# Moving the norm weight's scale, the last value products and the last block's output passes in a fused attention and feed-forward kernel

## What is computed

```python
x = x + _L0_xattn_ref(_layernorm(x), ctx_1024, mask, rms_scale, q_w, kv_w, out_w)   # cross attention over 1601 masked context rows
x = x + _L0_attn_ref(_layernorm(x), WQ, WK, WV, WO)                                 # causal self attention, 16 heads of 32
x = x + _L0_ffn_ref(_layernorm(x), W_fc, ln_w, ln_b, W_proj)
...
# _L0_ffn_ref
h = jnp.einsum('btd,hd->bth', x, absmean(W_fc))      # weights quantized to -1, 0, 1
h = jax.nn.gelu(h, approximate=False)
h = layernorm(h, ln_w, ln_b)                         # over 2048 features
return jnp.einsum('bth,dh->btd', h, absmean(W_proj))
```

## Time and profile before

| | us |
|---|---|
| median of 3 runs (lowest, highest) | 1093.79 (1090.33, 1094.54) |
| the profiled execution's own time | 1089.65 |
| its span | 1087.8 |
| PE busy in the span | 931.0 (86%) |
| DVE busy | 669.2 (62%) |
| ACT busy | 503.0 (46%) |
| POOL busy | 373.1 (34%) |

### The profile page before, as it was taken

The page is one execution under the profiler, slowest core; times in us unless marked ns, Lnnn a source line. Parts: engine busy times, 40 slices in busy tenths (PEclk is TensorE's granted clock), DMA queues, the critical chain, the costliest instruction groups (busy, mean ns, idle before and its releaser), DMA issues.

```text
span 1087.8 us, 22528 instructions
## 1 busy us (share of the span) xinstructions
PE 931.0 (86%) x7297; PEld 697.5 (64%) x7297; DVE 669.2 (62%) x1335; ACT 503.0 (46%) x1057; POOL 373.1 (34%) x500
## 2 busy tenths in 40 slices
PE   0898879898788888868879989998978999999995
PEld 0787757686667776657768878887754444444442
DVE  3587667766677766676266556766565447475543
ACT  2565445654455554535233233443445444556551
POOL 1354445444444444430012111221112334454533
PEclk9999999999999999979969999999988989999997
DMA  5532133221232322431355543443321202012011
GB/s 163 167 87 65 58 95 97 87 63 48 81 89 77 88 70 75 112 101 60 79 156 147 137 146 88 139 125 116 97 46 48 68 1 87 31 39 68 20 59 42
DMA packets 100608, 93.02 MB, mean 86 GB/s; under 512 B 45729, under 2 KB 62194, under 8 KB 100466
## 3 DMA queue, kind: packets, MB, share of 16 engines
q1 hardware_dynamic: 99856, 91.11, 28.9%
q10 hardware_dynamic: 578, 0.13, 0.1%
q0 software_dynamic: 32, 0.02, 0.0%
HBM read 74.37 MB, written 12.66 MB: 80 GB/s over the span
## 4 chain that ended last, share of the span: by engine, by line
PE 65%; DVE 14%; issue 10%; ACT 5%; ACTq 1%; DVEq 1%; POOL 1%; DMA 1%; SPq 1%; POOLq 0%
PE bank L245 44%; PE bank L1216 8%; PE bank L220 6%; PE bank L241 4%; DVE f L234 3%; DVE f L508 2%; ACT f L231 1%; DVEq L75 1%; ACTq L75 1%; PE bank L530 1%; ACT f L413 1%; DVE f L471 1%; DVE f L642 1%; DVE f L929 1%; PE bank L216 1%
## 5 line engine op out<-in xcount | busy, mean ns | idle before, releaser
L245 PE MATMUL bank<-f,f 128*128 128x256 f32 (+4 forms) x5032 | 635.4, 302 | 67.9 <-issue 26.3
L245 PEld LDWEIGHTS bank<-f,f 128*128 128x128 f32 (+3 forms) x5032 | 457.5, 162 | 195.7 <-issue 77.2
L220 PE MATMUL bank<-f,f 128*128 128x128 f32 x896 | 133.4, 280 | 60.1 <-DVE f L620 29.3
L234 DVE TENSOR_TENSOR f<-bank,f 128x512 fp32r<-128x512 f32 x211 | 140.7, 684 | 52.6 <-ACT f L231 50.6
L231 ACT ACTIVATE f<-bank 128x512 fp32r<-128x512 f32 x211 | 121.2, 592 | 85.6 <-PE bank L220 80.5
L220 PEld LDWEIGHTS bank<-f,f 128*128 128x128 f32 x896 | 103.6, 143 | 82.8 <-DVE f L620 31.1
L1194 POOL TENSOR_TENSOR f<-f,f 128x512 f32<-128x512 f32 x60 | 76.4, 1274 | 146.6 <-ACT f L1192 146.5
L1216 PE MATMUL bank<-f,f 128*128 128x512 f16 x512 | 124.9, 389 | 0.0
L1197 DVE SCALAR_TENSOR_TENSOR f<-bank,f,f 128x512 f16<-128x512 f32 x64 | 48.0, 750 | 107.0 <-ACT f L1184 73.5
L935 POOL TENSOR_TENSOR f<-f,f 128x512 f32<-128x512 f32 x32 | 33.4, 1045 | 182.8 <-DVE f L932 182.8
L469 POOL TENSOR_TENSOR f<-f,f 128x512 f32<-128x512 f32 x32 | 42.0, 1312 | 155.9 <-ACTq L75 133.2
(11 more groups left out here) (128 smaller groups left out, 989.0 us busy)
## 6 DMA issues: line engine op xcount, KB each, us to landing
f<-in_ctx_dram SPq DMA_DIRECT2D x71, 256.0 KB, 2.8
f<-x_scratch SPq DMA_DIRECT2D x64, 256.0 KB, 3.7
f<-in_x_dram SPq DMA_DIRECT2D x32, 256.0 KB, 3.2
x_scratch<-f SPq DMA_DIRECT2D x32, 256.0 KB, 2.1
f<-in_L_ffn_W_fc_dram SPq DMA_DIRECT2D x32, 256.0 KB, 2.8
f<-in_L_ffn_W_proj_dram SPq DMA_DIRECT2D x32, 256.0 KB, 3.5
f<-in_ktab_dram SPq DMA_DIRECT2D x71, 64.0 KB, 2.0
f<-f SPq DMA_DIRECT2D x64, 64.0 KB, 2.4
```

The costliest lines, as they stand in the source:

```text
L220: f = lambda e, i=i, a=a: e.transpose(dst[:, i, :], a, ident[0:rows, 0:rows])
L234: return maybe("dve", lambda e: e.tensor_tensor(lo, src, hi.bitcast(F32), ALU.subtract), sem(name + "_lo"), waits, when)
L245: f = lambda e, i=i, a=a, b=b: e.matmul(dst, a, b, start=(first and i == 0), stop=(last and i == n - 1), skip_group_check=check)
```

## The change

- `s3_scale` moves from slot H0-1 to slot B2+4 (order 4.6). Its small tiles move from a region that is free only late (`r`) into the constants, and its wait for that region goes to the steps that still use it (`s3_free`, `s3_rows`).
- The DVE step of `s3_apply` becomes a step of its own, `s3_turn`, at order 1.45 of the same slot: ahead of the strip's own DVE passes instead of behind them.
- For the last tile of self attention (i = 15), `s2_PV` keeps its slot s+4 = H0+6 but goes from order 0.5 to 2.6, behind strip 6 and the projection of strip 4; `s2_ET` goes to the next slot, behind strip 7; `s2_O` goes from slot s+5 to s+7.
- End: for the last strip the sum comes before the low half on DVE, and POOL's add of its squares goes; `s3_stat` of the last group adds them on PE with four more matmuls. Two tiles of strip 62's projection stand ahead of `s3_stat`, the other two behind it, then strip 63's four. For tiles 1 and 2 of the last group the first of the two DVE passes is done by ACT and POOL (`s3_mid`); the output passes go in the order of tiles 0, 3, 1, 2.

```diff
+    mrow, mdiag, isc, sc, lsc = const(2), const(2), const(2), const(2), const(2, 16)
...
-        at(s + 4, 0.5, lambda i=i: s2_PV(i))
+        at(s + 4, 0.5 if i < ni - 1 else 2.6, lambda i=i: s2_PV(i))
         at(s + 4, 0, lambda i=i: res_load(i))
-        at(s + 4, 5.5, lambda i=i: s2_ET(i))
-        at(s + 5 if i else s + 7, 5.6, lambda i=i: s2_O(i))
+        at(s + 4 if i < ni - 1 else s + 5, 5.5 if i < ni - 1 else 1.6, lambda i=i: s2_ET(i))
+        at(s + 5 if 0 < i < ni - 1 else s + 7, 5.6, lambda i=i: s2_O(i))
...
+    def s3_free():
+        tok["free"] = tok["qk", ni // 2 - 1]
+
+    def s3_turn(i):
+        u = i % 2
+        tok["tb", i] = op("dve", lambda e: e.scalar_tensor_tensor(rs2[:, u, 1:2], mv2[:, u, 0:1], -1.0, rs2[:, u, 0:1],
+                                                        ALU.mult, ALU.mult), sem("f_dv"), [tok["rs", i]])
+
     def s3_apply(i):
         u = i % 2
-        tb = op("dve", lambda e: e.scalar_tensor_tensor(rs2[:, u, 1:2], mv2[:, u, 0:1], -1.0, rs2[:, u, 0:1],
-                                                        ALU.mult, ALU.mult), sem("f_dv"), [tok["rs", i]])
...
-            tp = op("pool", lambda e: e.tensor_tensor(acc[:, v, 1, :], acc[:, v, 1, :], sq3[:, z, :], ALU.add),
-                    sem("f_acc2"), [ts, *tok["acc2", g]])
-            tok["acc2", g] = tok["sqr", z] = [tp]
+            if q == last:
+                tok["acc2", g] = [ts, *tok["acc2", g]]
+            else:
+                tp = op("pool", lambda e: e.tensor_tensor(acc[:, v, 1, :], acc[:, v, 1, :], sq3[:, z, :], ALU.add),
+                        sem("f_acc2"), [ts, *tok["acc2", g]])
+                tok["acc2", g] = tok["sqr", z] = [tp]
+        if q == last:
+            s3_sum(g, gp, [ts, th])
...
     def s3_plast():
+        for t in (2, 3):
+            s3_p(last - 1, [t])
         for t in range(4):
-            for q in (last - 1, last):
-                s3_p(q, [t])
+            s3_p(last, [t])
...
+                rows = slice(t * 128, (t + 1) * 128)
+                parts = [acc[:, v, z, rows]] + ([sq3[:, last % 2, rows]] if z and g == ng - 1 else [])
+                for n, a in enumerate(parts):
...
+    def s3_mid(j):
+        g = ng - 1
+        t = op("act", lambda e: e.activation(Po[:, j, :], sums[:, 0, :], ACT.Copy, scale=snm[:, j:j + 1]), sem("f_gelu"),
+               [*tok["nm3", g], *tok["sums"], *d2("fin", g - 1, j)])
+        tok["mid", j] = op("pool", lambda e: e.tensor_tensor(xr3[:, j, :], xr3[:, j, :], Po[:, j, :], ALU.add),
+                           sem("f_acc2"), [t, tok["xb", g * 4 + j]])
+
     def s3_fin(i):
         g, j = i // 4, i % 4
-        tb = op("dve", lambda e: e.scalar_tensor_tensor(xr3[:, j, :], sums[:, 0, :], snm[:, j:j + 1], xr3[:, j, :],
-                                                        ALU.mult, ALU.add), sem("f_dv"),
-                [tok["xb", i], *tok["nm3", g]])
+        if g == ng - 1 and j in (1, 2):
+            tb = tok["mid", j]
+        else:
+            tb = op("dve", lambda e: e.scalar_tensor_tensor(xr3[:, j, :], sums[:, 0, :], snm[:, j:j + 1], xr3[:, j, :],
+                                                            ALU.mult, ALU.add), sem("f_dv"),
+                    [tok["xb", i], *tok["nm3", g]])
...
+        at(s - 1, 1.45, lambda i=i: s3_turn(ni + i))
         at(s - 1, 1.55, lambda i=i: s3_apply(ni + i))
...
+            at(H0 + 16 * g + 18, 3 + 0.1 * j, lambda j=j: s3_mid(j) if j in (1, 2) else None)
+            at(H0 + 16 * g + 18, 4 + 0.1 * (0, 2, 3, 1)[j], lambda i=i: s3_fin(i))
...
+    at(H0 + last + 2, 2.1, lambda: s3_p(last - 1, [0, 1]))
...
-    at(H0 - 1, 4.6, s3_scale)
+    at(B2 + 4, 4.6, s3_scale)
+    at(H0 - 1, 4.6, s3_free)
```

More of the change, by code:

```diff
@@ L1122, in few @@
     ng = ni // 4
+    last = NF * ng - 1
     def s3_params():
@@ L1131, in s3_scale @@
         D_ = lambda f, w: op("dve", f, sem("f_dv"), w)
-        free = tok["qk", ni // 2 - 1]
-        tok["free"] = free
         for z, src in enumerate((lwp, lbp)):
@@ L1138, in s3_scale @@
         tk = op("pe", lambda e: e.transpose(bank[k][0:2, 0:128], mabs[:, :], ident[:, :]), sem("f_p"), [t, t_id, *gfree[k]])
-        t = D_(lambda e: e.tensor_reduce(mrow[0:2, 0:1], bank[k][0:2, 0:128], AX.X, ALU.max), [tk, *free])
+        t = D_(lambda e: e.tensor_reduce(mrow[0:2, 0:1], bank[k][0:2, 0:128], AX.X, ALU.max), [tk])
         t = D_(lambda e: e.tensor_scalar(mrow[0:2, 1:2], mrow[0:2, 0:1], 1.0 / 64, 1.0e-30, ALU.mult, ALU.max), [t])
@@ L1149, in s3_scale @@
         tok["lsc"] = ts
+    def s3_free():
[4 more added lines that the diff above has]
+                                                        ALU.mult, ALU.mult), sem("f_dv"), [tok["rs", i]])
     def s3_apply(i):
         u = i % 2
-        tb = op("dve", lambda e: e.scalar_tensor_tensor(rs2[:, u, 1:2], mv2[:, u, 0:1], -1.0, rs2[:, u, 0:1],
-                                                        ALU.mult, ALU.mult), sem("f_dv"), [tok["rs", i]])
         tok["xn", i] = [op("act", lambda e: e.activation(xn[:, u, :], xa[:, u, :], ACT.Identity, bias=rs2[:, u, 1:2],
-                                                         scale=rs2[:, u, 0:1]), sem("f_gelu"), [tb, *d2("xnT", i - 2)])]
+                                                         scale=rs2[:, u, 0:1]), sem("f_gelu"), [tok["tb", i], *d2("xnT", i - 2)])]
     def s3_T(i):
@@ L1201, in s3_h, with s3_sum @@
         if f == 0:
[L1202 to L1207, removed]
+            tok["acc", g] = [op("dve", lambda e: e.tensor_copy(acc[:, v, 0, :], gp), sem("f_dv"),
+                                [ts, th, *tok["free"], *d2("stat", g - 2)])]
+        elif q < last:
+            s3_sum(g, gp, [ts, th])
+        give(k, [tl, *tok["acc", g]])
+    def s3_sum(g, gp, waits):
+        a = acc[:, g % 2, 0, :]
+        tok["acc", g] = [op("dve", lambda e: e.tensor_tensor(a, gp, a, ALU.add), sem("f_dv"), [*waits, *tok["acc", g]])]
     def s3_p(q, tiles=range(4)):
@@ L1234, in s3_plast @@
     def s3_plast():
+        for t in (2, 3):
+            s3_p(last - 1, [t])
         for t in range(4):
-            for q in (last - 1, last):
-                s3_p(q, [t])
+            s3_p(last, [t])
     def s3_stat(g):
         v, k = g % 2, take()
+        w = [*tok["acc", g], *tok["acc2", g], *gfree[k], t_on]
         for t in range(4):
             for z in range(2):
[L1243 to L1246, removed]
+                rows = slice(t * 128, (t + 1) * 128)
+                parts = [acc[:, v, z, rows]] + ([sq3[:, last % 2, rows]] if z and g == ng - 1 else [])
+                for n, a in enumerate(parts):
+                    tk = op("pe", lambda e, t=t, z=z, a=a, n=n, m=len(parts) - 1: e.matmul(
+                        bank[k][:, z * 4 + t:z * 4 + t + 1], a, ones[:, 0:1], start=n == 0, stop=n == m,
+                        skip_group_check=True), sem("f_p") if t == 3 and z and n == len(parts) - 1 else None,
+                        w if t + z == 0 else ())
         tok["stat", g] = [tk]
@@ L1263, in s3_rows @@
             src = lsc[:, z, :]
-            t = op("dve", lambda e, z=z, src=src: e.tensor_copy(lwb[:, :, z], src), sem("f_dv"), [tok["lsc"]])
+            t = op("dve", lambda e, z=z, src=src: e.tensor_copy(lwb[:, :, z], src), sem("f_dv"),
+                   [tok["lsc"], *tok["free"]])
             for y in range(2):
@@ L1332, in few @@
         at(H0 + 16 * g + (13 if g else 17) + j, 4, lambda i=i: s3_base(i))
-        at(H0 + 16 * g + 18 + (j if g < ng - 1 else 0), 4 + j / 8, lambda i=i: s3_fin(i))
-    last = NF * ng - 1
+        if g < ng - 1:
+            at(H0 + 16 * g + 18 + j, 4, lambda i=i: s3_fin(i))
+        else:
+            at(H0 + 16 * g + 18, 3 + 0.1 * j, lambda j=j: s3_mid(j) if j in (1, 2) else None)
+            at(H0 + 16 * g + 18, 4 + 0.1 * (0, 2, 3, 1)[j], lambda i=i: s3_fin(i))
     for q in range(NF * ng):
```

2 lines of the change are left out of this document (1 added, 1 removed).

## The result

The changed kernel takes 1080.08 us (median of 4 runs, 1077.58 to 1082.13), the kernel before 1092.5 us (median of 4 runs beside it, 1090.33 to 1094.54): a ratio of 0.989, with a 95% interval of 0.987 to 0.992. That is 1.1% faster, where 0.62% was forecast: the right sign, inside the range, but a gain of some 12 us where 6.8 were worked out.

The account below looks back on a forecast made before the run. PE bounds the kernel (65% of the last chain), so waits count only where PE stands still. 3.8 - 5.1 - 4.8 - 0.7 = -6.8 us: 1082.9 for the profiled execution, 1087.0 for the median; range 1079 to 1093.

Parts of the forecast that it names:

- The scale into slot B2+4: First slots of self attention: the scale delays DVE's L234 and so PE's dense start; +3.8 us, bounds 0 and 6.
- Rival (a): First slots of self attention: the scale is hidden where it goes; -10.6 us in all, 1083.2; chance 0.14.
- The scale out of slot H0-1: Slot H0-1: PE waits only for the split, the clock still falls; -5.1 us, bounds 6.5 and 3.5.
- rival (b): Gaps move instead of closing, low clock stays two stretches at H0-1; -3.2 us in all, 1090.6; chance 0.2.
- The last value products: Slot H0+6: strip and projection fill PE's 4.94 us wait before the last tile's products; -4.8 us, bounds 3.5 and 6.5.
- The end: After the last strip: earlier sum, six DVE passes instead of eight, third held by POOL; -0.7 us, bounds 1.2 and -0.5.
- Rival (c): Groups 1 to 3: the turn waits for POOL's inverse root, holding strip passes 12 times; +7.6 us, 1101.4; chance 0.06.
- the seam: Between the first two groups, slots H0+17 to H0+22, with output passes on DVE; the forecast had no term there.

Follow-up runs that it names:

- turn back: The changed kernel with the small DVE step of the row norm behind the strip's two passes again: 1086.66 us, ratio to the kernel before 0.9952.
- the two experiments of the turn: The changed kernel with the turn behind the strip's passes again, 1086.66 us; the kernel before with only the turn moved ahead of them, 1086.12 us.
- turn only: The kernel before with nothing but the turn moved ahead of the strip's two passes: 1086.12 us, ratio to the kernel before 0.9946.
- scale back: The changed kernel with the scale back in slot H0-1, its tiles staying in the constants: 1081.25 us, ratio to the kernel before 0.9901.

## Why the prediction was right or wrong

**The scale into slot B2+4: right.** +3.8 forecast, +3.76 measured, with L1135 as the last thing that PE waits for and L234 late as worked out. The mechanism was shown by taking the scale away again (12.83) and by putting it elsewhere (12.82), and some 3.4 us of it are still there at H0-1. Rival (a), a hidden scale, is refuted.

**The scale out of slot H0-1: the mechanism right, the size off.** The stop of about 2.4 us came out at 2.57. The term went wrong in the length of the low clock: one short stretch was assumed (a loss of 1.4 us over the 20 matmuls), and the execution of after lost 2.8 (7.59 against 4.78). So the term is -3.40 instead of -5.1, just beyond its lower bound of 3.5 and as rival (b) had it for this place. With the turn back the same 20 matmuls took 6.10 us, a loss of 1.3; the forecast's size occurs, but the trace of before, with its 7.65, spoke for the other.

**The last value products: right**, with -5.2 for -4.8. No stop before the products, 1.37 us given back at the freed bank where 1.4 was forecast, both as worked out. The forecast expected 0.4 us of stop to remain.

**The end: right in its mechanism, and by luck in its sum**, -0.7 for -0.7. The third pass on DVE was held by POOL as forecast, for 0.4 us (1.14 against 0.75) where the forecast has about 0.5. DVE's last pass ended 1.0 us earlier where 0.7 was forecast, and the stores, for which the forecast has no term, took 0.3 back.

**What failed is the choice of places.** The prediction says "I read the timeline of each of the four places that the change touches", and prices the turn in one term, 1.2 us at the copy before the last value products; for a gain at any other place it has no term, and gives no reason. But the turn is a step of every tile of the norm, 12 of them in groups 1 to 3, and at one of these PE stood still for it: the stop of 2.07 us at 917.96, the second largest in PE's waits of the kernel before from 797 us on. With the fall of the clock behind it, it is worth 3.65 to 4.0 us, which the two experiments of the turn show from both sides. This term of the sum, put at nothing, is the step that failed. Rival (c) did look at the turn at all 12 places, but only for a loss. Against it, the prediction says that "the turn finds its root done", and that is wrong: in the kernel after the turn waits 0.37 to 0.94 us for POOL's inverse root at eight of the 12 places, and at two of these (910.71 and 969.85) it then takes 1.22 us itself. But no stop of PE shows behind any of them.

Without the seam the parts that were priced sum to 3.76 - 3.40 - 5.2 - 0.7 = -5.5, for which the forecast has -6.8. The seam adds -5.6. Of that, 1.64 us are not shown to be a part of the change. The clock falls beside the first group's column sums in every kernel, and the time from there to the next transposes is 14.0 to 14.3 us in five of the ten profiled executions and 15.7 to 16.0 in the other five. The turn's place does not divide them: with it behind the passes, before has the longer time and turn back the shorter one. The three executions with the scale at H0-1 (before, turn only, scale back) all have the longer time. Of the seven with it elsewhere, five have the shorter one, and the two in which the projection of tile 13 goes behind the first strip have the longer. So the move of the scale may have a part in it, or the moment at which the clock falls may be chance; one profiled execution of each kernel can't tell, and the cause is open.

So of some 12 us, 4.0 are the turn at the seam, 5.2 the value products with the turn's help, 0.7 the end, next to nothing the move of the scale as far as its two places show (3.76 paid, 3.40 saved), and 1.6 the moment of the clock's fall, with its cause open.

## What to carry to other kernels

Before pricing a move, read what the bounding engine waits for over the whole stretch in which the moved step recurs, and price the step at every repetition, for a gain as for a loss: an instruction of under 0.5 us cost 4 us because it stood behind two passes of a queue that PE waited for once. A stall that is moved to another place is worth only the difference of the queues that it meets; it is worth its full price (3.8 us here) when the step is cut up and placed where the engine it holds has other work. Where a stop can't be removed, fill it: eight matmuls put into a stop of 2.57 us gave back 4.6 us, more than the stop, because the clock stayed up.

## What the runs showed of the hardware

- Executions differ ahead of any change: up to the first value products of self attention, where the kernels do the same work, the profiled execution of after took 4.17 us longer. Its granted clock was 0.50 from 98 to 100, from 149 to 151 and from 159 to 161 us, where that of before was 1.00. In the eight experiments these value products begin between 547.32 and 552.54, so the lateness does not go with the change. A comparison by absolute times would have made it a cost of the change.
- The Trainium skill, page "SBUF — State Buffer", section "SBUF: two separate sides", says that a DVE operation with two SBUF inputs and a GpSimd operation that reads SBUF take turns, the later one waiting for the whole of the earlier. The prediction said that no row shows it for passes of 512 columns. The trace of before does: a pass L1310 at 907.86 took 1.77 us instead of 0.75, beside POOL's L1305 of 907.82 (1.27 us). The trace after agrees as well, in both directions: in the end fence, DVE's L1340 takes 1.14 us beside POOL's first add, and POOL's two adds take 1.27 and 1.71 us, the second of them held in its turn.
- The clock's fall can cost more than the stop ahead of it, and its price comes in two sizes here: behind stops of the same 2.57 or 2.58 us, the same 20 matmuls, which take 4.78 us at the full clock, took 7.39 to 7.59 us in four executions and 6.10 in one. What decides between the two was not tried.
